# First attention of a fused two-layer kernel: both halves of the value-weighted sums moved in front of the scores, with a weight-turning job, a key turn and several copies moved around them

## The reference, cut to what matters

```
x = x + tanh(g_xattn[0]) * mha(layernorm(x), ctx, ctx)     # 16 heads of 32, causal at the right edge
x = x + tanh(g_ffn[0])   * ffn(layernorm(x))               # Hadamard-rotated gated MLP
x = x + tanh(g_xattn[1]) * gqa(layernorm(x), ctx)          # 16 heads, 4 key/value heads of 128
x = x + tanh(g_ffn[1])   * self_attention(layernorm(x))

def mha(q, k, v):            # per head, k = v = the context's own 32 columns
    scores = q @ k.T / sqrt(32); scores = where(causal, scores, -10000)
    return softmax(scores) @ v
```

## Time and profile before

| | |
|---|---|
| median of 3 runs | 2027.46 us (2025.34 to 2031.85) |
| the profiled execution, its own time | 2025.43 us |
| its span, first to last instruction | 2023.7 us |
| mean granted TensorE clock | 0.992 |
| busy: PE / PEld / DVE / ACT / POOL | 96% / 80% / 62% / 57% / 42% |
| first stage (0 to 583 us): PE busy | 556.53 us |
| first stage: DVE / ACT / POOL busy | 415.45 / 382.24 / 269.48 us |

### The profile page before, as it was taken

One profiled execution on the slowest core, in us unless ns is written; L12 is line 12 of the kernel. 1 busy time (PEld: TensorE's weight loads), 2 busy tenths in 40 slices (PEclk: granted clock), 3 DMA queues, 4 the chain that ended last, 5 costly groups with the idle time before them and its releaser, 6 DMA issues. The chain is left out here.

```text
span 2023.7 us, 37397 instructions
## 1 busy us (share of the span) xinstructions
PE 1946.6 (96%) x13369; PEld 1623.8 (80%) x13369; DVE 1255.4 (62%) x2302; ACT 1152.3 (57%) x3032; POOL 850.6 (42%) x1010
## 2 busy tenths in 40 slices
PE   8999999999999999999989998899999999989997
PEld 6777777777778888898877886699999999877875
DVE  7777777776755643564435555666666666566665
ACT  6666666666653333453423445777777777454554
POOL 3525536445434000000003444888888788222222
PEclk9999999999999999999999998999999999999999
DMA  5426346344364210203003335334333433421101
GB/s 189 163 91 195 123 139 210 124 157 138 110 232 163 88 63 1 73 1 120 1 26 103 112 113 165 90 85 117 109 107 96 117 106 99 125 64 50 34 29 38
DMA packets 195370, 210.67 MB, mean 104 GB/s; under 512 B 60912, under 2 KB 135712, under 8 KB 194688
## 3 DMA queue, kind: packets, MB, share of 16 engines
q1 hardware_dynamic: 195200, 208.43, 32.8%
HBM read 128.43 MB, written 79.95 MB: 103 GB/s over the span
## 5 line engine op out<-in xcount | busy, mean ns | idle before, releaser
L1916 POOL TENSOR_TENSOR qd_rows<-qd_rows,c_rsum 112x375 f32<-112x375 f32 x256 | 202.4, 812 | 79.3 <-DVE c_rsum L2046 72.4
L2052 DVE TENSOR_TENSOR c_pT_lo<-c_turned,c_pT_hi 128x336 fp32r<-128x336 f32 x256 | 128.3, 502 | 125.2 <-ACT c_pT_hi L1991 125.2
L1982 ACT ACTIVATE qd_rows<-c_score,c_nmax 112x375 f32<-112x375 f32 x256 | 146.9, 574 | 86.8 <-DVE c_nmax L2041 86.8
L1347 ACT ACTIVATE b_silu<-b_gate,ab_scales 128x512 f32<-128x512 f32 (+1 forms) x64 | 40.7, 637 | 254.0 <-PE b_up L1476 254.0
L1413 DVE SCALAR_TENSOR_TENSOR b_hidden<-b_up,ab_scales,b_silu 128x512 f32<-128x512 f32 (+1 forms) x64 | 43.7, 683 | 196.5 <-ACT b_silu L1347 196.5
L539 ACT ACTIVATE a_probs<-a_score,a_nmax 112x375 f32<-112x375 f32 x256 | 144.2, 574 | 12.3 <-DVE a_nmax L712 12.3
L2346 POOL TENSOR_TENSOR f_probs<-f_probs,f_rsum 112x448 f32<-112x448 f32 x64 | 59.7, 933 | 202.3 <-DVE f_rsum L2470 202.3
L2041 DVE TENSOR_REDUCE c_nmax<-c_score 112x1 f32<-112x375 f32 x256 | 137.6, 538 | 0.4 <-PE c_score L2123 0.4
L985 PE MATMUL a_turned<-keep_ident,a_probs 112*128 112x112 f32 x768 | 123.0, 269 | 14.4 <-DVE a_pT L718 9.8
L2385 ACT ACTIVATE f_probs<-f_score,f_nmax 112x112 f32<-112x112 f32 x256 | 86.5, 364 | 80.6 <-DVE f_nmax L2465 80.6
L985 PEld LDWEIGHTS a_turned<-keep_ident,a_probs 112*128 112x128 f32 x768 | 85.3, 142 | 55.7 <-issue 21.7
(11 more groups left out here) (363 smaller groups left out, 5947.1 us busy)
## 6 DMA issues: line engine op xcount, KB each, us to landing
q<-q_qT SPq DMA_DIRECT2D x14, 1024.0 KB, 5.7
qd_raws<-q SPq DMA_DIRECT2D x64, 224.0 KB, 3.0
v<-bq_raw SPq DMA_DIRECT2D x48, 256.0 KB, 2.1
qd_raws<-v SPq DMA_DIRECT2D x64, 192.0 KB, 2.8
k<-bq_raw SPq DMA_DIRECT2D x16, 752.0 KB, 4.0
qd_raws<-k SPq DMA_DIRECT2D x64, 188.0 KB, 2.4
wug<-a_ug_turned SPq DMA_DIRECT2D x32, 256.0 KB, 2.3
bq_raw<-in_ctx_dram SPq DMA_DIRECT2D x15, 512.0 KB
```

What stands on the lines that cost most here:

```text
L1916: pool.tensor_tensor(probs[:, n % AHEAD, 0:T], probs[:, n % AHEAD, 0:T], rsum[:, n % (2 * H):n % (2 * H) + 1].broadcast_to([S, T]), ALU.mu ...
L1982: act.activation(probs[:, n % AHEAD, 0:T], score[n % AHEAD][0:S, 0:T], ACT.Exp, bias=nmax[:, c:c + 1], accum_out=sums[:, c:c + 1]).then_in ...
L2052: dve.tensor_tensor(pT[1][:, t % 2, :, j, :], src, f32(pT[0][:, t % 2, :, j, :]), ALU.subtract).then_inc(pT_split, 1)
```

## The change

Nothing is added to or taken from the work; instructions of `phase_a` change their places on PE, ACT and DVE. POOL's and SP's lists are the same, and so is the rest of the program.

```
             out_uses  (order in which the bank outp changes hands)
-            out_uses += [("keys", b, 0), ("job", b, 3), ("weigh", b, 0)] if cur else []
+            out_uses += [("keys", b, 0), ("weigh", b, 0), ("job", b, 3)] if cur else []

             ACT
+                    if n == 0 and before:
+                        copy_out(b - 1, HALVES - 1)          # was behind probs_copy
                     if n == 4 and cur:
-                        copy_job(b, 3)
+                        copy_out(b, 0)                       # was behind probs_copy
                         square_keys(b, 1)
                     if cur:
                         probs_copy(b, n)
+                    if n == 4 and cur:
+                        copy_job(b, 3)
                     if n == 0 and before:
-                        copy_out(b - 1, HALVES - 1)
-                    if n == 4 and cur:
-                        copy_out(b, 0)
+                        keys_out(b - 1, 2)                   # was behind exps

             DVE
-                    if n == 2 and cur:
-                        scale_keys(b, 0)
-                    if n == 6 and b >= 2 and cur:
-                        rotated_lo(b - 2)
                     if cur:
                         probs_copy(b, n)
+                    if n == 2 and cur:
+                        scale_keys(b, 0)
+                    if n == 6 and b >= 2 and cur:
+                        rotated_lo(b - 2)

             PE
+                    if n == 0 and before:
+                        weigh(b - 1, HALVES - 1)
+                    if n == 4 and cur:
+                        weigh(b, 0)
                     if n % 2 == 0:  scores(...)
                     if cur:
                         turn_probs(b, n, 0)
-                    if n == 0 and before:
-                        weigh(b - 1, HALVES - 1)
                     if n == 4 and cur:
-                        weigh(b, 0)
+                        run_job(b, 3)
+                        project(b, "v", 1, 0, 3)
                     if n == 0 and after:
                         turn_ctx(b + 1, 0)
+                    if n == 0 and before:
+                        turn_keys(b - 1, 2)
                     (turn_probs(b, n, 1))
                     if n == 4 and cur:
-                        project(b, "v", 1, 0, 6)
+                        project(b, "v", 1, 3, 6)
-                    if n == 0 and before:
-                        turn_keys(b - 1, 2)
                     if n == 3 and cur:
                         turn_keys(b, 0)
                         project(b, "k", 1, 6, 12)
-                        run_job(b, 3)
```

More of the change, by code:

```diff
@@ L645, in _ @@
                         act.activation(ab["scales"][:, 0:3 * IC], turned[:, 0:3 * IC], ACT.Copy)
-                    if n == 0 and before:
-                        keys_out(b - 1, 2)
                     if n == 1 and cur:
```

## The result

The changed kernel takes 2011.59 us (median of 4 runs, 2010.49 to 2014.57) against 2026.4 us (2024.0 to 2031.85) for the kernel before: ratio 0.9928, 95% interval 0.9914 to 0.9941. Forecast was 2012, with 2005 to 2021 around it. A later series gave 2011.6 and a ratio of 0.9923 (0.9910 to 0.9937).

A forecast was written before the change was run, and what follows sets the result against it. PE's instruction list in the first stage, at full clock, was taken as the bound. Terms 4.2 + 7.0 + 2.7 + 0 = 13.9 us off 2025.43 gave 2011.5, forecast as 2012 us, own range 2007 to 2017, outer range 2005 to 2021.

The forecast's parts named there:

- What bounds the kernel: First stage: PE works 556.53 of 583 us at full clock, so only shorter waits or cheaper switches on PE gain.
- Slots 2 and 3: DVE's probs_copy ahead of scale_keys: seven long-mark items gain 0.54 us each, down to a 4.08 floor; 4.2 us with last item.
- The last item's 0.4: Slot 3 of the last item: no next context, so no floor; gains about its own mark, 0.4 us.
- Slots 6 and 7: DVE's probs_copy ahead of rotated_lo: turn 0.60 us earlier, 0.10 given back at value projection; 0.50 in 14 items, 7.0 us.
- Slot 4: Sums, scores, turn, job on PE: cheaper switches gain 0.33 less 0.16 us, 0.17 in 16 items, 2.7 us.
- Slot 0: Sums ahead of scores on PE: switching gain used up by a new 0.2 to 0.3 us wait for DVE's copy; zero.
- The new mark by DVE's copy at the start of slot 1: Sign expected in the next profile: PE waits there for DVE's copy in most items, a new 0.2 to 0.3 us.
- The sum: All terms together: 4.2 + 7.0 + 2.7 + 0 = 13.9 us faster, off 2025.43: 2011.5 us.
- A: Rival, chance 0.12: slot 0 also gains because factors run fast, and switches are cheap; about 2004 to 2007 us.
- B: Rival, chance 0.12: the step from sums to scores is dear, 0.24 us more in 31 places, 7.4 us; 2019 us.
- C: Rival, chance 0.11: further unseen waits eat the freed time, slots 3 and 7 give only half; 2020 to 2022 us.
- D: Rival, chance 0.05: later scores in slots 0 and 4 make turns starting slots 1 and 5 wait for DVE; 2033 us.

## Why the prediction was right, point by point

- **What bounds the kernel** (PE's list, in full clock): right. The gains on PE came out at the end of the stage: 14.8 us by slots, 14.6 over the fifteen stretches, 15.4 at the second stage's start with 0.7 that are not the change's.
- **Slots 2 and 3, 4.2 us** with a floor at 4.08 by `values_out`: right, 0.54 per long item, nothing for the short ones. Alone it gave 3.8 us. The last item's 0.4 was wrong: no context turn stands there, but the projection came only 0.14 earlier.
- **Slots 6 and 7, 7.0 us**: the mechanism was right, two small terms were off and nearly cancel. Key turn to turn of probabilities is 0.44 and not the 0.36 that I had from key turn to projection; and the 0.10 given back at the value projection didn't occur. 0.55 and not 0.50 in 13 items; the 14th, the last, kept 0.10 of it. Alone 6.9 us.
- **Slot 4, 2.7 us**: mis-sized. The entry into the sums after a projection is 0.10 (1.02 to 1.03 against 0.92), and sums to scores is 1.29, both as taken. But turns that follow a turn of probabilities take 0.34 and not 0.28 behind the scores, and slot 5 gives back 0.05. 0.09 to 0.12 per item, 1.4 to 1.9 us, by distances alone; the time can't show it.
- **Slot 0, nothing**: this term was wrong, by 2.4 us. I let DVE's way there be 3.82 (start of the factors, 0.78 for them, 0.50, 0.14) and PE's own 3.48. The factors took 0.57 in the median, and the copy starts 0.08 before their recorded end, so DVE's way is 2.92 + 0.49 + 0.14 = 3.55; PE's own work is 3.62. The new mark by DVE's copy at the start of slot 1, which I forecast for most items, is in none of them. The step that failed is the duration: I knew the two values and the lock behind them, kept the slow value, and did not work out which of POOL's operations the factors would meet. POOL's run starts from DVE's `sum_keys` in slot 7, not from the scores. The sums ahead of the scores put the scores, and the factors 2.39 behind them, 1.29 later against that run; the swap in slot 6 takes 0.41 of it back. With the first alone (the trace of PE's and ACT's moves) the factors take 0.23 or 0.24 us in 14 of 16 items; with the second alone 0.32 to 0.39 from the third to the fifteenth, with both 0.54 to 0.61, and before the change most took 0.74 to 0.78. That cover is all but used up there was right: 0.05 us are left.
- **The sum** agrees better than its terms: 13.9 us forecast, 14.6 to 14.8 measured. Slot 0's 2.4 too few and the 1.3 too many in slot 4, with some 0.8 too many for the last item, nearly cancel, and that was luck.
- **Rivals.** A was half right: slot 0 kept its gain, the switches were not cheaper. B fell: sums to scores is 1.29. The rule of the Trainium skill (TensorE: Matmul & The Clock Gate, "Part 3: Packing small matmuls — row/col tiling"), by which the scores' weight load would wait for the sums, shows no price of its own here: the scores follow after the same 1.29 as turns do. C and D didn't occur; the run with ten extra instructions shows what D would look like and its price, 0.24 for 0.29 of delay.

## What to carry to other kernels

Before pricing a wait, look at what stands right behind the waiting instruction and work out when that could start: of two marks of 0.9 and 0.26 the second was worth nothing, since the next instruction had a floor of its own. A wait that is gone can also bring forward another: in the last item both did. The name on a mark is a guess, and its length is too short where ends are modelled: the marks of 0.26, 0.36 and 0.91 here were 0.43, 0.52 and 1.07 by distance to the changed kernel; the copy that ends 0.14 us before PE starts is the releaser, and distances from start to start are the size. In an order written by hand, put the instruction that frees a shared bank ahead of one that itself waits; and when a block is moved out of a stretch, check both engines' ways through what is left.

## What the runs showed of the hardware that I had not expected

- A 16-column factor multiply on VectorE took 0.23 to 0.78 us in the kernel before; wherever it took over 0.25, its end followed the end of a GpSimd operation by 0.03 us. In the changed kernel 0.53 us of other work in front of it moved nothing on PE.
- A turn of probabilities behind four turns of 128 columns starts after 0.44 us, a projection behind the same after 0.36.
- The second stage's first transposes ran slower, in a stretch where the granted clock fell, in some traces of kernels with the same code there (394 against 259 ns each in the changed kernel and the kernel before), right after a pause of 2.0 us on PE between the stages. The granted clock of the first 2 us there was 0.50, the 1.2 GHz level, in the changed kernel and 0.87 in the kernel before:

```profile
L1510 PE MATMUL b_y<-keep_ident,bq_xin x4: 394/394/419, 567.4 to 567.9; 112*128 112x112 f32 x4
```
